# The first attention's values products in pairs of groups, and its output stages one step later

## What is computed

```
x = x + L0_attn_a(layernorm(x))   # 16 heads of 8, rotary q and k, softmax
x = x + L0_ffn(layernorm(x))      # silu(gate) * up, 384 hidden
x = x + L0_attn_b(layernorm(x))   # 16 heads of 8, causal, sparsemax
x = x + L0_ffn(layernorm(x))      # the same weights
# in each attention, for each head:
#   out = probs(q k^T) @ v
```

## Time and profile before

| what | value |
|---|---|
| median of 3 runs | 621.91 us (621.61 to 622.36) |
| the profiled execution, its own time | 621.83 us |
| its span | 618.7 us |
| TensorE, VectorE, ScalarE, GpSimd busy | 94%, 78%, 68%, 63% of the span |
| granted TensorE clock, mean | 0.985 |
| first `take_out` of soft items, last one | 76.1 us, 339.6 us |

### The profile page before, as it was taken

The page is one execution under the profiler, slowest core; times in us unless marked ns, Lnnn a source line. Parts: engine busy times, 40 slices in busy tenths (PEclk is TensorE's granted clock), DMA queues, the critical chain, the costliest instruction groups (busy, mean ns, idle before and its releaser), DMA issues.

```text
span 618.7 us, 19166 instructions
## 1 busy us (share of the span) xinstructions
PE 582.1 (94%) x6716; PEld 451.5 (73%) x6716; DVE 484.8 (78%) x1421; ACT 422.8 (68%) x1057; POOL 389.7 (63%) x824
## 2 busy tenths in 40 slices
PE   5897999999999999999999999999999999999984
PEld 4674556767777776777677888778888888888663
DVE  2298778888888888987787888887888888899332
ACT  1113667778777777778787777767777877777762
POOL 4745446677776667777666766676666666653341
PEclk9999999999999999999999999989999999999997
DMA  3587577765666655545444445432655544440000
GB/s 93 137 238 183 127 165 173 165 168 149 149 154 149 151 134 136 144 119 136 132 124 131 122 124 116 117 82 76 138 115 124 120 108 123 117 124 21 12 10 21
DMA packets 74439, 76.23 MB, mean 123 GB/s; under 512 B 10276, under 2 KB 68836, under 8 KB 69732
## 3 DMA queue, kind: packets, MB, share of 16 engines
q1 hardware_dynamic: 74340, 74.97, 48.7%
HBM read 46.86 MB, written 23.33 MB: 113 GB/s over the span
## 4 chain that ended last, share of the span: by engine, by line
PE 67%; DVE 15%; issue 5%; ACT 4%; POOL 4%; DMA 3%; SPq 0%; POOLq 0%; ACTq 0%; DVEq 0%
PE banks L1501 14%; PE banks L1455 9%; PE banks L1479 8%; PE banks L1432 7%; PE banks L1371 6%; DVE top L1102 4%; PE banks L1423 3%; DVE top L1101 3%; PE banks L1458 3%; PE banks L1403 2%; PE banks L1424 2%; DVE neg_shift L1096 2%; ACT probs_t L1291 2%; PE banks L1482 2%; PE banks L1381 2%
## 5 line engine op out<-in xcount | busy, mean ns | idle before, releaser
L1291 ACT ACTIVATE probs_t<-banks 128x512 f32<-128x512 f32 (+1 forms) x512 | 266.9, 551 | 79.2 <-PE banks L1479 51.6
L1096 DVE TENSOR_REDUCE neg_shift<-banks 128x2 f32<-128x512 f32 x256 | 166.1, 681 | 42.4 <-PE banks L1455 41.2
L1501 PE MATMUL banks<-probs_t,v_ext 128*32 128x256 f32 (+1 forms) x2048 | 118.9, 361 | 0.1
L1455 PE MATMUL banks<-k_stack,q_stack 72*128 72x256 bf16 x512 | 99.8, 276 | 8.4 <-DVE neg_shift L1096 2.9
L1102 DVE MAX8 top<-banks 128x8 f32<-128x256 f32 x256 | 105.6, 413 | 0.0
L1479 PE MATMUL banks<-q_stack,k_stack 75*128 75x256 bf16 x512 | 98.8, 274 | 0.2
L987 POOL TENSOR_TENSOR hidden<-up_tanh,gate_half 128x256 f32<-128x256 f32 x96 | 70.0, 732 | 43.6 <-DVE up_tanh L1142 38.2
L1101 DVE MAX8 top<-banks 128x8 f32<-128x128 f32 x256 | 74.1, 290 | 26.3 <-PE banks L1464 25.3
L1501 PEld LDWEIGHTS banks<-probs_t,v_ext 128*32 128x32 f32 x2048 | 55.9, 110 | 39.1 <-issue 14.6
L1455 PEld LDWEIGHTS banks<-k_stack,q_stack 72*128 72x128 bf16 x512 | 41.3, 98 | 46.9 <-DVE neg_shift L1096 33.1
L1458 PE MATMUL banks<-k_stack,q_stack 128*128 128x128 bf16 x256 | 56.6, 221 | 6.2 <-DVE top L1102 4.6
(11 more groups left out here) (108 smaller groups left out, 1387.2 us busy)
## 6 DMA issues: line engine op xcount, KB each, us to landing
q_stack<-q_image SPq DMA_DIRECT2D x96, 192.0 KB
k_stack<-k_image SPq DMA_DIRECT2D x96, 192.0 KB
q_image<-qk_parts SPq DMA_DIRECT2D x32, 192.0 KB, 2.3
k_image<-qk_parts SPq DMA_DIRECT2D x32, 192.0 KB, 2.1
q_image<-qk_parts SPq DMA_DIRECT2D x32, 128.0 KB, 2.2
o_image<-out_t SPq DMA_DIRECT2D x32, 128.0 KB, 1.9
out_compact<-o_image SPq DMA_DIRECT2D x32, 64.0 KB
rdenominators<-r_image SPq DMA_DIRECT2D x16, 128.0 KB, 2.5
```

Source lines behind the costliest of these rows:

```text
L1096: dve.tensor_reduce(m.nm[:, n % STACKS, h, :], scores.rearrange("p (q k) -> p q k", q=TT), AX.X, ALU.max, negate=True).then_inc(reduced, 1)
L1291: act.activation(m.pt[:, (n * Q + g) % GROUPS, i, 0:size], shifted_banks[:, j % 2, 0:size], ACT.Exp if is_soft(n) else ACT.Relu, scale=SCA ...
L1455: ins = pe.matmul(scores[:, qt * T:(qt + 1) * T], qs[0:STACK, h, qt * P:(qt + 1) * P], ks[0:STACK, h, :], start=True, stop=True)
L1501: ins = pe.matmul(out_bank[32 * i:32 * i + 32, at + skip:at + T], v_windows(v, kt)[:, Q * g + i, :], m.pt[:, (n * Q + g) % GROUPS, i, kt * ...
```

## The change

The soft items take the plain items' form: groups 0 and 1 at step 40 of the item, groups 2 and 3 at step 48. `take_out` moves from 49 to 50, `store_out` from 50 to 51 and `load_out` from 53 to 54; the first of these is used by plain items too. No matmul, no DMA and no wait is added or taken away.

```
-          pass2=30, pv=36, pv_pairs=40, take_out=49, store_out=50, load_out=53, invert=57, store_rden=57, load_rden=60,
+          pass2=30, pv_pairs=40, take_out=50, store_out=51, load_out=54, invert=57, store_rden=57, load_rden=60,
...
-                n, g = divmod(step - AT["pv"], H)
-                if 0 <= n < B and g % Q == 0:
+                n, g = divmod(step - AT["pv_pairs"], H)
+                if 0 <= n < ITEMS and g % (2 * Q) == 0:
                     if n == 0 and g == 0:
                         pe.wait_ge(bias_ready, 2)
-                    pv(n, g // Q)
-                n, g = divmod(step - AT["pv_pairs"], H)
-                if B <= n < ITEMS and g % (2 * Q) == 0:
                     pv(n, g // Q)
                     pv(n, g // Q + 1)
```

## The result

The changed kernel took 644.56 us (median of 4 runs, 639.33 to 647.65), the kernel before beside it on the same chip 622.13 (4 runs, 621.61 to 622.93): a ratio of 1.036 (95% interval 1.0322 to 1.0398), 22.4 us slower. The forecast was 636.0, with a range of 628 to 640: slower was right, the time fell outside.

A forecast was written before the change was run, and what follows sets the result against it. The prediction took VectorE, not TensorE, to pace steps 1 to 7. Soft items added 10.1 + 1.5 + 0.7 + 0 + 1.0 and plain items 0.8, together 14.1, on 621.9: 636.0 us, range 628 to 640.

The forecast's parts named there:

- What bounds the kernel: Soft stretch: VectorE paces steps 1 to 7; head 5's reduction ends 0.04 before step 7's scores, despite TensorE busy 20.00 of 20.
- What a group and a pair cost: Values products on TensorE: a group 1.11 us in all, a pair's second group adds 0.87; TensorE work saved 0.48 per item.
- Steps 1 to 8: Half stretch: losing step 4's group buys nothing, the pair at step 8 is 0.87 longer, so +0.87 us.
- Steps 9 to 0: Other half stretch: losing step 12's group wins 0.82, the pair at step 0 gives 0.87 back, net +0.05 us.
- The moved stages: Later output stages: `take_out` hidden or delaying ScalarE 0.3 until about step 4; price 0, at worst 0.3 per item.
- The 0.8 for the plain half: Plain half: moved `take_out` delays the gates by 0.3, taken as 0.05 per item, 0.8 us for 16 items.
- The sum of the order: Soft half: the items' added costs from regrouping, 0.92 us each for items 3 to 13, other amounts at the ends.
- items 1 and 2: Early soft items: item 1 costs 0.7, its first half swallowed by the denominators' wait; item 2 costs 1.5 us.
- items 12 to 15: Late soft items: 12 and 13 cost 0.92 each; 14 and 15, beside plain scores, 1.0 us for both.
- The clock: Rival: TensorE's standstills drop the clock once per stretch, 16 x 1 us or more, over 650; chance 0.04.
- TensorE as the bound: Rival: TensorE is the bound after all, so the 0.48 per item is gained, giving 614; chance 0.07.
- ScalarE catching `up1`: Rival: ScalarE holds VectorE's run up by up to 0.3 per soft item, and as much in plain ones, 641; chance 0.08.

The follow-up runs named there:

- VectorE and ScalarE relieved and single groups: Kernel before with reductions over 256 of 512 columns and, from item 1, activations of 256 of 512: 616.77 us, ratio 0.9922.
- filler kernel: Changed kernel plus eight small identity-weight matmuls per soft item in TensorE's openings at steps 4, 5 and 7: 638.97 us, ratio 1.0281.
- the stages unmoved and filler present: Changed kernel with output stages put back where they were, plus the eight small matmuls per soft item: 634.27 us, ratio 1.0235.
- the same again: Changed kernel, unedited, run again beside the kernel before on a later chip: 641.35 us, ratio 1.0314.
- halved reductions: Changed kernel with the soft half's maximum reductions reading 256 of 512 score columns: 634.69 us, ratio 1.0216.
- the changed kernel with both engines relieved: Changed kernel with half of each reduction and, from item 1, half of each activation: 625.19 us, ratio 1.0068.

## Why the prediction was right in direction and wrong in size

**What bounds the kernel: right.** VectorE paces step 7. Step 7's scores stay 5.33 to 5.38 behind step 1's with a group between them, with nothing, and with filler. They aren't fixed to the hundredth: 5.22 with both pairs and the output stages unmoved, 5.60 with the stages alone moved. And the lead is narrow: with VectorE and ScalarE relieved and single groups it is 5.23. The row of 20.00 busy out of 20 misled about the direction, as the prediction said. The Trainium skill (Perfetto Trace Analysis, Identifying the Most-Contended Engine) says that matmul busy share is not a good measure of how close TensorE is to its limit; the trace agrees, since eight more matmuls per item left the stretch at 18.87.

**What a group and a pair cost: right,** 1.86 measured for 1.87.

**Steps 1 to 8, +0.87: right.** 0.85 by the pair of groups 0 and 1 alone, 0.82 in the changed kernel. **Steps 9 to 0, +0.05: right.** -0.03 by the other pair alone, 0.05 in the changed kernel. Both together, stages unmoved, +0.75.

**The moved stages, price 0: wrong.** ScalarE's 0.3 was seen, and step 4's shifted scores come where the prediction put them (232.00 - 229.10 = 2.90). That `up1` would just not be caught was wrong. In the changed kernel `gate_half`, for whose end `up1` waits, ends at 233.33 and `up1` starts at 233.36, 4.26 behind step 1's scores. In the kernel with both pairs and the stages unmoved `gate_half` ends 0.2 before `up1`, which starts at 4.15 (step 1's scores at 233.87). The `gate_half` of the changed kernel, then that of both pairs and its `up1`:

```profile
232.85 0.48 ACT L1317 ACTIVATE gate_half<-banks 128x256 f32<-128x256 f32 x1
...
237.35 0.45 ACT L1317 ACTIVATE gate_half<-banks 128x256 f32<-128x256 f32 x1
...
238.02 0.41 DVE L1142 SCALAR_TENSOR_TENSOR up_tanh<-gate_tanh,banks 128x256 f32<-128x256 f32 x1
```

The prediction took 4.32 for `up1` from the kernel before, where `a_var_eps` ahead of it took 0.42 (at 237.58); in the kernel with both pairs it takes 0.24, and so `up1` was due earlier than 4.32. The price is 0.11 to 0.12 per stretch beside the pairs, and 0.2 with single groups. By the end of the soft half it is 2.7 us, most of it outside the steady stretches; alone, the moved stages cost 1.1% of the time. Pairs and stages come to 18.87, +0.87 for the forecast 0.92: the two misses nearly cancel. The 0.8 for the plain half was too much: from the last soft to the last plain `take_out` it is 259.1, and was 259.0.

**The sum of the order: 15.6 in the soft half, for 13.3 forecast.** From the marks of the filler kernel against those of before, except that for items 12 to 15 the unedited kernel's are taken, where filler itself costs 0.9:

| part | forecast | measured |
|---|---|---|
| item 0 | 0 | 0.9 |
| items 1 and 2 | 0.7 + 1.5 | 1.0 + 1.4 |
| item 3 | 0.9 | 1.1 |
| items 4 to 11 | 7.4 | 7.2 |
| items 12 to 15 | 2.8 | 4.0 |

Item 0's 0.9 may be clock: the filler kernel's profile has 6.8 us at the lower clock there, that of before 3.4. In items 12 to 15 the moved stages are part of it: with the stages unmoved and filler present the four give 3.8, with moved stages 4.9. The runs with one change each split it: the pair of groups 0 and 1 alone costs 1.4 in the four, where four steady stretches would cost 3.4, so that step 4 wins some there was right; the pair of groups 2 and 3 alone costs 1.8, and nothing in a steady stretch; the stages alone cost 1.4. Why the second pair costs 0.4 per item here stays open.

**The clock: the step that failed.** The sum has no term for it, so the clock stood at nothing. 621.9 + 15.6 = 637.5 would have been inside the range; what lies above is the clock's. The rival was priced all or nothing, "once per stretch", at over 650, given 0.04 and argued away with one row of the plain half (18.76 of 20 at 1.00). The same trace of the kernel before holds a fall 30 us further on (length, busy times, clock, DMA):

```profile
406.00:407.00 1.00, 0.68 (x8) 0.45 (x6) 0.87 (x4) 1.00 (x4) 0.92 (x2) 1.00 0.00 0
407.00:408.00 1.00, 0.35 (x7) 0.35 (x8) 1.00 (x5) 0.55 (x2) 0.90 (x3) 1.00 0.02 4
...
409.00:410.00 1.00, 1.00 (x7) 0.94 (x7) 1.00 (x4) 0.57 (x2) 0.85 (x3) 0.50 0.14 38
```

So gaps in TensorE's work were followed by the lower clock in this kernel too, and the row chosen was one where they weren't. What happened in the changed kernel lies between none and all: a fall in some stretches only, 1.6 us each in the steady half, more in items 0 to 2. In the profiled execution 20.5 us more than in the filler kernel were spent at the lower level; at half speed that loses 10.3, and its marks are 365.61 - 356.09 = 9.5 behind, 10.4 with the 0.9 that filler costs. By the ratios filler gives back 0.3% with moved stages, within the intervals, and 1.1% with stages unmoved. What the order's 15.6 leaves of the 22.4 is 6.8, and from 2 (the run of 639.33) to 10 (that of 647.65) by the run. This is a remainder and not a measurement. An estimate from the mean clocks, 0.972 in the middle of the four runs and 0.985 in the profiled execution before, gives (1 - 0.972) x 641 - (1 - 0.985) x 618.7 = 8.7 if all of it cost TensorE's time.

That the openings bring the falls rests on this: between 80 us and the last soft `take_out`, five of the seven profiles of kernels whose step 4 has lost its group, without filler, show at least one fall (the changed kernel 4, the same again 2, the pair of groups 0 and 1 alone 1, halved reductions 1, both pairs with unmoved stages 3; the changed kernel with both engines relieved, and the pairs at steps 6 and 14, none). None of the other seven does: before, groups 2 and 3 alone, stages alone, both engines relieved with single groups, groups 2 and 3 at step 14, and the two with filler. It is one profile each. Which stretch is hit, no run here explains.

The other rivals: TensorE as the bound is out, by the filler kernel. ScalarE catching `up1` did happen, by 0.11 of the 0.3 that the rival allowed, and ScalarE is one of the two next limits once VectorE is relieved. A cure by a third score bank, so that VectorE could work ahead under a block, wasn't tried.

## What to carry to other kernels

Before moving filler-like work (values products, projections) together, measure the start times of what stands behind it against the end of what releases it: if they coincide, that work was covering another engine's pace, and the block that it joins will idle that engine for its whole length less what its buffers hold. Then look through the whole trace for openings that the clock fell behind, not only for one that it didn't. Price the openings that are left behind twice: as waits, and as places where the clock may fall in a part of the executions, which deserves its share of the range and not an all-or-nothing case.

## What the runs showed of the hardware

- The same opening doesn't always bring the clock down. In the changed kernel steps 4 to 7 looked alike in all steady stretches, and 3 of them fell in one execution and none in another. In the kernel before, the plain half has two neighbouring microseconds with TensorE busy for 0.46 and 0.64 (378 to 380 us), at a granted clock of 1.00, and 406 to 409 us with 0.68, 0.35 and 0.61, after which the clock was at its lower level for 3.4 us.
- VectorE's `TENSOR_SCALAR` of two columns took 0.17 us in one stretch and 0.78 in the next, ending with GpSimd's `TENSOR_TENSOR` that started 0.01 after it. With halved reductions alone it took 0.74 to 0.76 in seven of the eight stretches from 133 to 263 us. The Trainium skill (SBUF — State Buffer, SBUF: two separate sides) has VectorE and GpSimd share one pair of ports as an exclusive lock, for some of VectorE's operations; these rows would fit, but no experiment here separated the two engines or shows that this operation takes the shared pair.
- The kernel before, unedited, ran from 616.71 to 626.83 us over the three sets of runs on the later chips, 1.6% apart, against 0.2% on the first chip: this kernel's times are told apart only by many runs or by the marks inside the trace.
